# Helical rotation bias: from bias matmuls to a bias operand in the squares and in the normalisation

## The chip, the core and the metric

The kernel runs on one core of a Trainium2 chip. TensorE does matmuls (its results go to PSUM), VectorE and ScalarE do elementwise work on PSUM and SBUF, GpSimd does elementwise work on SBUF alone, and SyncE (SP) starts the DMA transfers. The metric is the device time of the core in microseconds; lower is better. Line numbers (L955) are those of the profiled kernel.

## What is computed

The reference is a stack of two small transformer layers on 1024 tokens of 128 features. The change lies in one of its six blocks, the helical attention of the second layer:

```python
qh = (x @ Wq.T + bq).reshape(b, s, h, hd)          # 16 heads of 8 features; kh the same
q_hel = einsum('bshd,hed->bshe', qh, Whel) + bhel  # 64 helical features a head
n = sqrt(sum(q * q, axis=-1, keepdims=True))       # q_hel taken as 32 pairs; k_hel the same
qn = q / maximum(n, 1e-12)
helical = einsum('bhpsc,bhptc->bhst', scramble(qn), scramble(kn)) / 32
dot = einsum('bshd,bthd->bhst', qh, kh) / sqrt(hd)
attn = softmax(0.5 * dot + 0.5 * helical)
out = einsum('bhst,bthd->bshd', attn, vh) ... @ Wo.T + bo
```

What counts here is `+ bhel` on the rotation's result, the sum of the two squares of a pair, the bound 1e-12 on the norm (1e-24 on its square), and the product with the inverse norm.

## The kernel before

All engines run programs written out by hand; each engine does its instructions in the order of its program, and semaphores join them. No scheduler sets an order. The 1024 tokens are two halves of 512 columns. A bank is one of the eight 128x512 float32 regions of PSUM.

The helical attention runs in eight **turns** `u = 0..7` (`HEL`: half `u // 4`, group of four heads `u % 4`) and two more to drain. In turn u:

- TensorE (the loop under `for u in range(len(HEL) + 2)`): `dots(u, w)` for query and key, then `rotate(u, w, j)` for four **rotations** n = 4u + 2w + j. A rotation fills bank `2 + n % 4` with two halves of 256 columns, c = 0 and 1, the two features of a pair. Each half is one matmul for the bias (L661) and three (`mm3`, L326 to L328) for the product, since each operand is split into a high and a low part for float32 accuracy. Then come the transposes of the softmax weights of turn u-2, the first score product of u-1 (`score`, L683), work for values or projections, the weighing of values for u-2 (L710), and the second score product of u-1. A rotation waits for the bank's last reader (`h_norm`).
- ScalarE: the query's dot bias (L991), the softmax exponential of u-2 (L997), `squares(2u)` and `squares(2u+1)` (L955, a bank each, four in all), `inverse(2u)` (L960 a logarithm, L961 an exponential with scale -0.5: the inverse norm), a copy of turned weights (L1010), `inverse(2u+1)`, and half of the score extraction (L970).
- GpSimd: `add_squares(m)` (L1140), the sum of a pair's squares, once for each of m = 2u and 2u+1; once, in turn 3, the low part of the second half's tokens (`y_rest`, L1096) stands between the two. Before the turns it makes the high and low parts of the weights (L1129, L1132), and ahead of those the memsets for the bias matmuls (L1119 to L1123).
- VectorE: `mask_dot` (L1539, L1540), `softmax_sum` (L1587), `normalise(2u)` (L1564, four STT: scalar-tensor-tensor, which take the smaller of the inverse norm and a bound and multiply by the rotation in PSUM), half of the score extraction (L1549), `normalise(2u+1)`, work for values (L1572) or projections (L1525), `result(u-2)` (L1599), the second extraction, and `softmax_shift(u-1)` (L1580 the maximum, L1582 the subtraction) which releases L997 of the next turn.

The bias comes by DMA as a 34-row tile `hbias` (16 x 128 numbers, each row pair twice) into `wraw` at L294. VectorE splits it into high and low rows (`stage_bias`, L1499 and L1500, in the decoder's first sum), and the bias matmul multiplies those rows, in the zeroed tiles `ph` and `pl`, by rows of ones. The bound of the norm lies in two places: the logarithm's bias `lntiny` (1e-26 after a scale of 2^20) and the minimum with 1e12 in L1564.

## Time and profile before

| | us |
|---|---|
| median of 3 runs (lowest to highest) | 568.51 (567.17 to 570.62) |
| the profiled execution, its own time | 567.71 |
| its span | 565.9 |
| TensorE busy, matmuls | 455.4 (80%) |
| VectorE busy | 421.8 (75%) |
| ScalarE busy | 301.6 (53%) |
| GpSimd busy | 102.3 (18%) |
| helical attention, first rotation to its last result | about 314 to 430 |

The span is what the hardware profiler recorded of one execution; 1.8 us lie around it. Busy time is time in which an engine has an instruction in flight. Instructions of one engine overlap a little: two neighbours' starts may be closer than one's duration, and the start-to-start time is what a row of equal instructions costs each. An entry "xN" in a timeline is N neighbours merged, its time from the first start to the last end. A note in brackets is the idle time ahead of the instruction and the instruction that ended it. "L1564 <- L961" in a list of waits means that the first sat idle for the second.

### The profile page before, as it was taken

What the parts mean: (1) busy time and instruction counts of PE and PEld (TensorE: products, weight loads), DVE (VectorE), ACT (ScalarE), POOL (GpSimd) and SP (SyncE); (2) the same over time, 40 slices, a digit from 0 to 9 for tenths busy, and PEclk for the clock granted to TensorE, in tenths of its full rate; (3) what the DMA queues carried; (4) which work ended last, traced back from release to release, by engine and by line L of the source; (5) the groups of instructions that cost most, each with busy time, mean ns of one, the idle gap of its engine ahead of it and who ended that gap; (6) DMA issues with size and microseconds to landing.
All of it is one profiled execution on the core that took longest, in us unless ns stands there. A gap on an engine that the chain in (4) does not pass through costs nothing.

```text
span 565.9 us, 9003 instructions
## 1 busy us (share of the span) xinstructions
PE 455.4 (80%) x2936; PEld 343.3 (61%) x2953; DVE 421.8 (75%) x1022; ACT 301.6 (53%) x567; POOL 102.3 (18%) x106
## 2 busy tenths in 40 slices
PE   5883327999999999475686979999865579999996
PEld 2442314778778787352344868888754337777774
DVE  3489865777777777668877796778687667888885
ACT  4252134667776675332233567765642227777774
POOL 1000030122211120070000221321100502222220
PEclk9887557999999999757888899999995659999999
DMA  8950001111011100000000000000001110211101
GB/s 311 415 209 0 0 7 50 57 57 56 9 47 56 56 15 2 0 0 2 1 1 2 1 2 2 1 2 2 2 1 38 38 37 1 68 44 37 37 1 37
DMA packets 7566, 24.08 MB, mean 43 GB/s; under 512 B 790, under 2 KB 3014, under 8 KB 7404
## 3 DMA queue, kind: packets, MB, share of 16 engines
q1 hardware_dynamic: 7532, 23.63, 11.5%
q8 instruction: 20, 0.33, 0.2%
q14 instruction: 14, 0.11, 0.1%
HBM read 23.11 MB, written 0.52 MB: 42 GB/s over the span
## 4 chain that ended last, share of the span: by engine, by line
PE 60%; DVE 21%; issue 7%; ACT 6%; DMA 3%; SPq 2%; POOL 1%; DVEq 0%; ACTq 0%; POOLq 0%
PE pair L326 14%; PE pair L327 13%; PE pair L328 13%; DMA arena<-in_zT 3%; PE turn L320 2%; DVE arena L1564 2%; PE pair L683 1%; PE turn L326 1%; DVE work L1382 1%; PE turn L474 1%; PE pair L609 1%; DVE st L1190 1%; ACT YT L807 1%; DVE Y L1213 1%; PE turn L327 1%
## 5 line engine op out<-in xcount | busy, mean ns | idle before, releaser
L326 PE MATMUL pair<-yTh,wh 128*128 128x512 f32 x128 | 61.4, 480 | 4.1 <-issue 3.8
L1047 ACT ACTIVATE work<-pair,vec 128x512 f32<-128x512 f32 x64 | 44.1, 689 | 29.5 <-PE pair L328 24.2
L1671 DVE TENSOR_TENSOR pair<-work,turn 128x512 f32<-128x512 f32 x64 | 44.5, 696 | 17.9 <-ACT work L1047 16.1
L327 PE MATMUL pair<-yTl,wh 128*128 128x512 f32 x128 | 51.9, 405 | 0.0
L328 PE MATMUL pair<-yTh,wl 128*128 128x512 f32 x128 | 51.6, 403 | 0.0
L1419 DVE TENSOR_TENSOR pair<-work,pair 128x512 f32<-128x512 f32 x48 | 33.4, 696 | 23.3 <-PE pair L328 22.0
L1103 POOL TENSOR_TENSOR wl<-wraw,wh 128x512 fp32r<-128x512 f32 x24 | 30.9, 1291 | 97.5 <-ACT wh L878 97.5
L899 ACT ACTIVATE ph<-pair 128x512 fp32r<-128x512 f32 x48 | 28.8, 600 | 27.0 <-DVE pair L1419 27.0
L886 ACT ACTIVATE work<-pair 128x512 f32<-128x512 f32 x64 | 38.3, 598 | 4.5 <-PE pair L328 3.4
L326 PE MATMUL pair<-ph,wh 128*128 128x512 f32 x96 | 38.3, 399 | 0.9 <-DVE pl L1437 0.8
L683 PE MATMUL pair<-arena 64*128 64x128 f32 x512 | 32.9, 278 | 6.3 <-ACT work L970 4.6
L328 PE MATMUL pair<-ph,wl 128*128 128x512 f32 x96 | 37.9, 395 | 0.0
L327 PE MATMUL pair<-pl,wh 128*128 128x512 f32 x96 | 37.8, 393 | 0.0
L1564 DVE SCALAR_TENSOR_TENSOR arena<-work,pair 128x256 f32<-128x256 f32 x64 | 22.6, 416 | 19.1 <-ACT work L961 18.9
L683 PEld LDWEIGHTS pair<-arena 64*128 64x128 f32 x512 | 29.9, 188 | 9.0 <-ACT work L970 6.1
L1140 POOL TENSOR_TENSOR work<-work 128x512 f32<-128x512 f32 x16 | 20.4, 1279 | 76.5 <-ACT work L955 76.5
L320 PE MATMUL turn<-con,Y 128*128 128x128 f32 x56 | 13.0, 379 | 26.1 <-DVE Y L1213 19.6
L1437 DVE TENSOR_TENSOR pl<-pair,ph 128x512 fp32r<-128x512 f32 x48 | 32.8, 684 | 0.1
L807 ACT ACTIVATE YT<-turn 128x512 f32<-128x512 f32 x16 | 9.6, 597 | 43.1 <-PE turn L320 43.1
L1096 POOL TENSOR_TENSOR yTl<-YT,yTh 128x512 fp32r<-128x512 f32 x6 | 7.7, 1278 | 134.9 <-ACT yTh L821 134.9
L326 PEld LDWEIGHTS pair<-yTh,wh 128*128 128x128 f32 x128 | 25.4, 199 | 9.9 <-issue 5.6
L328 PEld LDWEIGHTS pair<-yTh,wl 128*128 128x128 f32 x128 | 24.9, 194 | 6.2
(285 smaller groups left out, 1200.3 us busy)
## 6 DMA issues: line engine op xcount, KB each, us to landing
wraw<-in_w SPq DMA_DIRECT2D x8, 768.0 KB, 4.4
arena<-in_zT SPq DMA_DIRECT2D x8, 514.0 KB, 10.8
arena<-in_z SPq DMA_DIRECT2D x8, 512.0 KB, 11.4
wraw<-in_w SPq DMA_DIRECT2D x8, 512.0 KB, 3.2
mat<-in_mat SPq DMA_DIRECT2D x1, 2312.0 KB, 17.9
row<-in_row SPq DMA_DIRECT2D x1, 576.0 KB, 17.3
X<-in_x SPq DMA_DIRECT2D x1, 512.0 KB, 4.1
out_x<-X SPq DMA_DIRECT2D x2, 256.0 KB, 2.5
```

What stands on the lines that cost most here:

```text
L326: pe.matmul(out, ah, bh, start=start, stop=False)
L327: pe.matmul(out, ah, bl, start=False, stop=False)
L328: return pe.matmul(out, al, bh, start=False, stop=stop)
L683: last = pe.matmul(pair[2][:, j, (2 * i + k) * P:(2 * i + k + 1) * P], a[rows, cols], b[rows, cols], start=n == 0, stop=n == 1, skip_group ...
L886: act.activation(act_out[q % 2], GATE0, ACT.Silu).then_inc(m["act"], 1)
L899: act.activation(ph[q % 2][:, :], UP0[q % 4], ACT.Copy).then_inc(m["hi"], 1)
L1047: act.activation(act_out[q % 2], UP1[q % 4], ACT.Relu, bias=vec[:, bass.ds(at, 1)])\
L1103: pool.tensor_tensor(wl[k][:, cols], wraw[:, cols], wh[k][:, cols].bitcast(F32), ALU.subtract)\
L1419: dve.tensor_tensor(up, act_out[q % 2], up, ALU.mult).then_inc(m["mul"], 1)
L1437: dve.tensor_tensor(pl[q % 2][:, :], UP0[q % 4], ph[q % 2][:, :].bitcast(F32), ALU.subtract)\
L1564: last = dve.scalar_tensor_tensor(out, inv, (QF, 1.0)[m % 2] * 1e12, src, ALU.min, ALU.mult)
L1671: dve.tensor_tensor(UP1[q % 4], act_out[q % 2], bank[h], ALU.mult).then_inc(m["mul"], 1)
```

## The change

The bias no longer passes through TensorE. A new tile `bhel` (128 x 16) holds it as columns, one for each rotation half. Two DMA loads of 4-byte pieces fill it at the start, on SP's queue between the parameters and the first expert weights. ScalarE squares each half of a bank by itself, with `bhel`'s column as the activation's bias; VectorE's STT adds the same column to the rotation and multiplies by the inverse norm. The bound of the norm is a maximum with 1e-24 on GpSimd behind each sum of squares, with a semaphore `h_sum2` between the two. The bias matmuls, their staging on VectorE, their memsets on GpSimd, `lntiny` and the old load are gone.

```diff
+            for r, c, n in ((0, 0, W0C // P), (32, W0C // P, NH - W0C // P)):
+                sp.dma_start(bhel[:, c:c + n], d["hbias"][r, 0:n * P].rearrange("(k p) -> p k", p=P),
+                             allow_slow_non_contiguous=True).then_inc(bias_loaded, 16)
...
-                    sp.dma_start(wraw[0:34, :], d["hbias"]).then_inc(bias_loaded, 16)
...
                 for c in range(2):
-                    bias, one = hel_bias(2 * pr + c)
                     o = bank[2 + n % 4][:, c * 256:(c + 1) * 256]
-                    pe.matmul(o, bias, one, start=True, stop=False)
                     last = mm3(o, whel(wh, 2 * pr + c), whel(wl, 2 * pr + c), qe_h(h, w)[:, cols], qe_l(h, w)[:, cols],
-                               False, True)
+                               True, True)
...
                     act.wait_ge(h_hel, n + 1)
-                    act.activation(sq(m)[:, j * HN:(j + 1) * HN], bank[2 + n % 4], ACT.Square).then_inc(h_sq, 1)
+                    for c in range(2):
+                        at = j * HN + c * 256
+                        last = act.activation(sq(m)[:, at:at + 256], bank[2 + n % 4][:, c * 256:(c + 1) * 256],
+                                              ACT.Square, bias=hel_bias(n, c))
+                    last.then_inc(h_sq, 1)
...
-                step(act.activation(n2(m), n2(m), ACT.Ln, scale=float(2 ** 20), bias=lntiny[:, :]))
+                step(act.activation(n2(m), n2(m), ACT.Ln, scale=float(2 ** 20)))
...
-            for b in bias_at:
-                pool.memset(b[:, :].bitcast(F32), 0.0)
-            pool.memset(ones[:, :].bitcast(F32), 0.0).then_inc(pool_step, 1)
-            pool.wait_ge(pool_step, 2)
-            for r in (0, 32):
-                pool.memset(ones[r:r + 2, 8 * r:8 * r + 256].bitcast(F32), 1.0).then_inc(bias_zero, 1)
...
                 pool.tensor_tensor(n2(m).rearrange("p (j m) -> p j m", j=2), s4[:, :, 0], s4[:, :, 1], ALU.add)\
-                    .then_inc(h_n2, 1)
+                    .then_inc(h_sum2, 1)
+                pool.wait_ge(h_sum2, m + 1)
+                pool.tensor_scalar(n2(m), n2(m), 1e-24, None, ALU.max).then_inc(h_n2, 1)
...
-            def stage_bias():
-                dve.wait_ge(bias_loaded, 16)
-                dve.wait_ge(bias_zero, 2)
-                for c, b in enumerate(bias_at):
-                    raw = wraw[0:34, c * HN:(c + 1) * HN]
-                    step(dve.tensor_copy(b[0:34, :], raw))
-                    last = dve.scalar_tensor_tensor(b[0:34, :], b[0:34, :].bitcast(F32), ccol("biaslo")[0:34, :], raw,
-                                                    ALU.mult, ALU.add)
-                last.then_inc(h_bias, 1)
...
-                        last = dve.scalar_tensor_tensor(out, inv, (QF, 1.0)[m % 2] * 1e12, src, ALU.min, ALU.mult)
+                        last = dve.scalar_tensor_tensor(out, src, hel_bias(n, c), inv, ALU.add, ALU.mult)
```

ScalarE and VectorE wait for the two loads once, ahead of the turns. What stands on ScalarE in turn 3, from the softmax exponential to the second inverse step, before:

```order
L997 ACTIVATE work<-work 128x512 [waits h_sub]
L955 ACTIVATE work<-pair 128x512 [waits h_hel,h_n2]
L955 ACTIVATE work<-pair 128x512 [waits h_hel]
L955 ACTIVATE work<-pair 128x512 [waits h_hel,h_n2]
L955 ACTIVATE work<-pair 128x512 [waits h_hel]
L960 ACTIVATE work<-work,lntiny 128x512 [waits h_n2]
L961 ACTIVATE work<-work,cq 128x512 [waits act_step]
```

and now, in the same turn:

```order
L999 ACTIVATE work<-work 128x512 [waits h_sub]
L954 ACTIVATE work<-pair,bhel 128x256 [waits h_hel,h_n2]
L954 ACTIVATE work<-pair,bhel 128x256
L954 ACTIVATE work<-pair,bhel 128x256 [waits h_hel]
L954 ACTIVATE work<-pair,bhel 128x256
L954 ACTIVATE work<-pair,bhel 128x256 [waits h_hel,h_n2]
L954 ACTIVATE work<-pair,bhel 128x256
L954 ACTIVATE work<-pair,bhel 128x256 [waits h_hel]
L954 ACTIVATE work<-pair,bhel 128x256
L961 ACTIVATE work<-work 128x512 [waits h_n2]
L962 ACTIVATE work<-work,cq 128x512 [waits act_step]
```

Four squares have become eight, and the logarithm has lost its bias operand. On GpSimd, from the first sum to the end of the sums, before:

```order
L1140 TENSOR_TENSOR work<-work 128x512 [waits h_sq] x2
L1140 TENSOR_TENSOR work<-work 128x512 [waits h_norm,h_sq] x5
L1096 TENSOR_TENSOR yTl<-YT,yTh 128x512 [waits y_hi]
L1140 TENSOR_TENSOR work<-work 128x512 [waits h_norm,h_sq] x9
L1096 TENSOR_TENSOR yTl<-YT,yTh 128x512 [waits y_hi] x2
```

and now, around turn 3:

```order
L1134 TENSOR_TENSOR work<-work 128x512 [waits h_norm,h_sq]
L1137 TENSOR_SCALAR work<-work 128x512 [waits h_sum2]
L1097 TENSOR_TENSOR yTl<-YT,yTh 128x512 [waits y_hi]
L1134 TENSOR_TENSOR work<-work 128x512 [waits h_norm,h_sq]
L1137 TENSOR_SCALAR work<-work 128x512 [waits h_sum2]
```

Each sum has a maximum behind it, and every later instruction of GpSimd stands behind both.

## Rows read from the trace of the kernel before

**Rows 1.** Windows: us, then busy us (instructions) of PE, PEld, DVE, ACT, POOL; PEclk.

```profile
367.00:380.00 13.00, 12.46 (x179) 11.22 (x177) 10.69 (x30) 8.14 (x15) 2.37 (x3) 1.00 0.01 3
...
407.00:420.00 13.00, 10.34 (x137) 9.30 (x137) 8.59 (x22) 7.82 (x15) 2.56 (x2) 1.00 0.01 1
```

**Rows 2.** Waits, 310 to 430 us: total us, times, longest.

```profile
DVE arena L1564 <- ACT work L961: 18.9, 9, 3.8
```

**Rows 3.** Timeline of VectorE, turn 4: start, us, instruction [idle before].

```profile
363.77 0.69 DVE L1582 TENSOR_TENSOR work<-work,hstat 128x512 f32<-128x512 f32 x1
...
369.04 1.42 DVE L1564 SCALAR_TENSOR_TENSOR arena<-work,pair 128x256 f32<-128x256 f32 x4 [2.14 <-ACT work L961]
370.37 0.84 DVE L1549 COPY work<-pair 32x256 f32<-32x256 f32 x2
371.24 1.42 DVE L1564 SCALAR_TENSOR_TENSOR arena<-work,pair 128x256 f32<-128x256 f32 x4
...
374.16 1.17 DVE L1599 TENSOR_TENSOR Y<-turn,hstat 32x128 f32<-32x128 f32 x4
...
376.96 0.69 DVE L1582 TENSOR_TENSOR work<-work,hstat 128x512 f32<-128x512 f32 x1
```

**Rows 4.** Timeline of ScalarE, turn 4.

```profile
364.49 0.63 ACT L997 ACTIVATE work<-work 128x512 f32<-128x512 f32 x1 [1.50 <-DVE work L1582]
365.03 1.73 ACT L955 ACTIVATE work<-pair 128x512 f32<-128x512 f32 x3
367.05 0.60 ACT L955 ACTIVATE work<-pair 128x512 f32<-128x512 f32 x1 [0.29 <-PE pair L328]
367.54 0.71 ACT L960 ACTIVATE work<-work,lntiny 128x512 f32<-128x512 f32 x1
368.29 0.72 ACT L961 ACTIVATE work<-work,cq 128x512 f32<-128x512 f32 x1
```

**Rows 5.** Timeline of GpSimd, turns 3 and 4.

```profile
354.46 1.29 POOL L1096 TENSOR_TENSOR yTl<-YT,yTh 128x512 fp32r<-128x512 f32 x1
...
366.18 1.28 POOL L1140 TENSOR_TENSOR work<-work 128x512 f32<-128x512 f32 x1 [9.20 <-ACT work L955]
367.72 1.27 POOL L1140 TENSOR_TENSOR work<-work 128x512 f32<-128x512 f32 x1 [0.26 <-ACT work L955]
```

**Rows 6.** Timeline of TensorE, the last rotation of turn 4.

```profile
366.37 0.29 PE L661 MATMUL pair<-pl,ph 128*128 128x256 f32 x1
366.49 0.28 PE L326 MATMUL pair<-arena_r,wh 128*128 128x256 f32 x1
```

**Rows 7.** Timeline of ScalarE, turn 2: an activation of 128x256 with a bias column.

```profile
346.34 0.84 ACT L977 ACTIVATE arena_r<-turn,vec 128x256 fp32r<-128x256 f32 x2
```

**Rows 8.** Timeline of VectorE, turn 2: an STT with a column, from PSUM.

```profile
347.21 0.88 DVE L1525 SCALAR_TENSOR_TENSOR arena_r<-turn,vec,arena_r 128x256 fp32r<-128x256 f32 x2 [0.41 <-ACT arena_r L977]
```

**Rows 9.** Groups of GpSimd by line and form: busy us, mean ns, idle us before.

```profile
L1158 POOL CAST wh<-wraw 128x512 fp32r<-128x512 f32 x16 | 9.4, 616 | 69.2 <-PE pair L328 65.6 <-DMA wraw<-in_w 3.6
```

**Rows 10.** Timeline of ScalarE, turn 6.

```profile
392.74 2.04 ACT L955 ACTIVATE work<-pair 128x512 f32<-128x512 f32 x4
395.19 0.72 ACT L960 ACTIVATE work<-work,lntiny 128x512 f32<-128x512 f32 x1 [0.41 <-POOL work L1140]
```

**Rows 11.** Timeline of ScalarE and VectorE, turn 7.

```profile
408.25 0.60 ACT L955 ACTIVATE work<-pair 128x512 f32<-128x512 f32 x1 [0.29 <-PE pair L328]
...
410.24 1.42 DVE L1564 SCALAR_TENSOR_TENSOR arena<-work,pair 128x256 f32<-128x256 f32 x4 [3.25 <-ACT work L961]
```

**Rows 12.** Timeline of VectorE, turn 0.

```profile
321.28 2.91 DVE L1564 SCALAR_TENSOR_TENSOR arena<-work,pair 128x256 f32<-128x256 f32 x8 [2.55 <-ACT work L961]
```

**Rows 13.** Timeline of ScalarE, decoder's second half.

```profile
296.02 0.28 ACT L814 ACTIVATE ry<-mv,eps 128x4 f32<-128x4 f32 x1
```

**Rows 14.** The line L878: duration min/median/max in ns, first and last start.

```profile
L878 ACT ACTIVATE wh<-wraw x24: 612/624/634, 79.0 to 203.3; 128x512 fp32r<-128x512 f32 x24
```

**Rows 15.** The page, part 2: DMA busy in tenths, 40 slices.

```profile
DMA  8950001111011100000000000000001110211101
```

More of the change, by code:

```diff
@@ L101, in build @@
         omt, tdn, step_bias = sb("omt", [P, 3]), sb("tdn", [P, 1]), sb("step_bias", [P, 2])
-        hstat, lntiny = sb("hstat", [P, 48]), sb("lntiny", [P, 1])
+        hstat, bhel = sb("hstat", [P, 48]), sb("bhel", [P, NH])
         eps = sb("eps", [P, 1])
@@ L194, in build, with hel_bias @@
         vb = lambda t: vb_at[t]
-        bias_at, ones = [ph[0], ph[1], pl[0]], pl[1]
-        def hel_bias(k):
-            r, c = (0, k) if k < 12 else (32, k - 12)
-            return blk(bias_at[c // 4], c % 4), ones[:, 8 * r:8 * r + 256]
+        def hel_bias(n, c):
+            pr = 2 * HEL[n // 4][1] + n % 2
+            return bhel[:, 2 * pr + c:2 * pr + c + 1]
         def own_banks(rows):
@@ L237, in build @@
         f_h, f_relu, f_out, f_sum = (sem("f_" + n) for n in ("h", "relu", "out", "sum"))
-        h_w, bias_loaded, h_bias, bias_zero = sem("h_w"), sem("bias_loaded"), sem("h_bias"), sem("bias_zero")
-        h_e, h_eh, h_ec, h_hel, h_sq, h_n2, h_inv, h_norm, h_d, h_dq, h_dk, h_v, h_vb = (
-            sem("h_" + n) for n in ("e", "eh", "ec", "hel", "sq", "n2", "inv", "norm", "d", "dq", "dk", "v", "vb"))
+        h_w, bias_loaded = sem("h_w"), sem("bias_loaded")
+        h_e, h_eh, h_ec, h_hel, h_sq, h_sum2, h_n2, h_inv, h_norm, h_d, h_dq, h_dk, h_v, h_vb = (
+            sem("h_" + n) for n in ("e", "eh", "ec", "hel", "sq", "sum2", "n2", "inv", "norm", "d", "dq", "dk", "v", "vb"))
         h_s, h_sxa, h_sxd, h_sub, h_exp, h_sum, h_et, h_ets, h_pv, h_o, h_out, h_x = (
@@ L740, in _ @@
             pe.wait_ge(h_w, 1)
-            pe.wait_ge(h_bias, 1)
             for u in range(len(HEL) + 2):
@@ L981, in _ @@
             copy_turned(yt(0))
+            act.wait_ge(bias_loaded, 32)
             for w in range(2):
@@ L1074, in _ @@
             pool.memset(cq[:, :], LN2 * 10 + math.log(QF))
-            pool.memset(lntiny[:, :], 1e-26)
             pool.memset(eps[:, :], EPS).then_inc(eps_ready, 1)
@@ L1117, in _ @@
             pool.wait_ge(tok_ready, 8)
-            for b in bias_at:
-                pool.memset(b[:, :].bitcast(F32), 0.0)
-            pool.memset(ones[:, :].bitcast(F32), 0.0).then_inc(pool_step, 1)
-            pool.wait_ge(pool_step, 2)
-            for r in (0, 32):
-                pool.memset(ones[r:r + 2, 8 * r:8 * r + 256].bitcast(F32), 1.0).then_inc(bias_zero, 1)
-            pool.wait_ge(bias_zero, 2)
             parts = [(wh[0][:, :], wl[0][:, :], mcol("Whel", 0, W0C)),
@@ L1129, in _ @@
                 pool.tensor_copy(hi, w).then_inc(pool_step, 1)
-            pool.wait_ge(pool_step, 6)
+            pool.wait_ge(pool_step, 5)
             for hi, lo, w in parts:
@@ L1508, in decoder_sum @@
                 step(dve.tensor_tensor(v, v, along("b2"), ALU.add))
-                if h == 0:
-                    stage_bias()
                 dve.wait_ge(f_out, h + 1)
@@ L1610, in add_out @@
                 dve.tensor_tensor(half(X, h), bank[1], half(X, h), ALU.add).then_inc(h_x, 1)
-            dve.wait_ge(h_bias, 1)
+            dve.wait_ge(bias_loaded, 32)
             for u in range(len(HEL) + 2):
```

## Prediction

> **What bounds the kernel now.** I read the page's 40 slices first, to find the stage that the change touches. The helical attention runs from about 310 to 430 us of the 565.9 us span; everything else in the diff is a load at the start, a little work of GpSimd and VectorE in the stages before. The stage is eight turns u = 0..7 (two halves of the tokens times four groups of heads), and from turn 3 on a turn takes about 13.1 us. The busy time by stretch [rows 1] says TensorE: 12.46 of 13.00 us busy in turn 4, at full clock. By that alone, taking matmuls away looks like a gain. But a busy TensorE can be one that is paced by others, so I then read who waits, and VectorE waits 18.9 us in nine waits for one thing, ScalarE's second step of the inverse norm (L961) [rows 2]. So I walked one turn on each engine.
>
> On VectorE [rows 3] the turn closes into a loop. The softmax shift L1582 ends at 364.46 (363.77 plus 0.69). Normalising of the next unit, L1564, starts at 369.04, after 2.1 us of idle time; between them lie only 2.5 us of other work. Then come four STT (1.33 to the next start), two copies (0.87), four STT (1.33), the value blocks, the result (L1599), two copies, the maximum and the shift again, which ends at 377.65: 13.19 later, with nothing idle from 369.04 on. What fills the 4.58 us from shift to normalising is ScalarE [rows 4]: exponential L997 at 364.49, squares L955 from 365.03, the fourth square at 367.05, logarithm L960 at 367.54, exponential L961 at 368.29 to 369.01. Two paths end at that logarithm together. One is TensorE's: the fourth square waited 0.29 for the last rotation. The other is GpSimd's: the sum of the first two squares ran from 366.18 to 367.46 [rows 5], 0.08 before the logarithm. In turn 6 ScalarE's squares run without a wait and the logarithm waits 0.41 for GpSimd [rows 10]. So there are three ties: TensorE, ScalarE's queue and GpSimd each set the turn to within 0.3 us.
>
> **TensorE: 64 bias matmuls go.** Starts of neighbours are 0.12 apart (366.37, 366.49) [rows 6], so a turn loses 8 x 0.12 = 0.95 us of TensorE, 7.6 us in all. Only the fourth square waits for that, and it is 0.3 us before the next bound. I take nothing for it in turns 3 to 6, where the path below gets longer than TensorE's.
>
> **ScalarE: each square becomes two halves with a bias operand.** The nearest row has exactly this shape, PSUM to SBUF, 128x256, bias from a column: two of L977 take 0.84 with 0.47 for one [rows 7], so start to start is 0.37. GpSimd needs the first four halves: 3 x 0.37 + 0.47 = 1.58 us from the first start. Before, two whole squares took about 1.08 (2.04 for four less two further steps of 0.48 [rows 10]). That is **+0.50** ahead of GpSimd. All eight take 3.06 against 2.04, or 2.6 with the wait for TensorE. Bounds: a half costs no less than half a whole square's 0.56 (then +0.05 in place of 0.50) and no more than 0.47 with no overlap (+0.8).
> The Trainium skill ("ScalarE: Activation LUTs", What ACT_TABLE_LOAD costs) states that a [128,1] pointer operand adds about 93 ns to an activation, with a fixed part besides the time per element and 93 ns of overlap back to back; by it a half would be about 0.49 with 0.40 start to start, an estimate, and this term +0.6. The trace's 0.47 and 0.37 nearly agree, and the sum goes by the trace.
> The logarithm loses its bias operand. Same size without one is L997's 0.63, against L960's 0.71 [rows 4]: **-0.08** on the path.
>
> **GpSimd: a maximum behind each sum.** The trace has no such operation. One input, one output, 128x512 is the cast L1158 at 0.61; two inputs is the sum itself, 1.28 [rows 5, 9]. I take 0.61, since the maximum against a constant has one input like the cast, and 0.08 for the wait on the engine's own semaphore: **+0.69**. Upper end 1.28 + 0.08. Nothing excludes a little less than the cast, but the same tile must be read and written, so I keep it as the lower end.
> The Trainium skill ("GPSIMD Engine Reference", 4.1 Engine selection) says that elementwise work such as a maximum belongs on VectorE, since two-input operations are some two times slower on GpSimd, while one-input ones run roughly at line rate. Here the rows show 1.28 against VectorE's 0.69 for two inputs, as it says, and 0.61 for one. Taken as one-input the sum keeps 0.69; taken as two-input it would be 1.36.
> Queued behind the maximum is the next sum. Sum, maximum, sum, maximum end 2.22 + 2 x (1.26 + 0.69) = 6.1 after the shift; logarithm 2 and exponential 2 then end at 7.6. VectorE wants that at 5.66 + 1.60 + 0.87 = 8.1. So the second inverse stays hidden, except in turn 3, where the remainder of y (L1096, 1.24 [rows 5]) stands between the two sums: there it comes at 8.9 and VectorE waits 0.8. Before, that turn lost about 0.5 at the same place, so +0.3.
>
> **VectorE: normalising takes a bias column.** L1564 runs at 0.335 start to start (1.42 for four with 0.42 for one) [rows 3]. L1525 is an STT of 128x256 with source PSUM, a column and an SBUF tensor, the new form: 0.88 for two with 0.48 for one [rows 8], so 0.40. Eight per turn, all on the loop: 8 x 0.065 = **+0.52**. Lower end 0; upper 0.6.
>
> **The sum for a turn.** In turns 4, 5 and 6: 0.50 + 0.69 - 0.08 + 0.52 = 1.6 us each, 4.9 in all. Check that nothing gained on TensorE comes off: its last rotation now ends 0.95 earlier relative to VectorE's result, and ScalarE's last half runs from about 3.2 after the shift, when TensorE has long delivered, so TensorE now idles. Turn 3: 1.6 + 0.3 = 1.9. The first turns have no softmax ahead of the squares, and the squares waited for TensorE each time, so TensorE's gain pays for ScalarE's halves there. What is left in turn 0 is the second inverse: VectorE's eight STT ran in one piece, 2.91 from 321.28 [rows 12]; now, by the prices above, the first sum starts near 317.8, the second maximum ends near 321.8, the inverse at 323.2, and the last STT ends 0.8 later. Turn 1 hides more, turn 2 adds 0.2 (its last square is late by 0.75 on ScalarE behind the copy of turned tokens, of which most is carried over): 1.0 together. Turn 7 was TensorE's: the fourth square at 408.25 waited for it, normalising began at 410.24 [rows 11]. With 0.95 less there, ScalarE's halves end at 408.3, GpSimd's maximum at 408.8, so the start stays, but eight slower STT remain: +0.5. Sum: 1.0 + 1.9 + 4.9 + 0.5 = **+8.3 us**.
>
> **Elsewhere: nothing.** VectorE loses six staging instructions in the decoder's first sum, but what follows waits for ScalarE's L814, which at 296.02 starts with no idle time behind a relu [rows 13]: it can't come sooner because its input does. At most 0.1. GpSimd loses six memsets ahead of the weights' high and low parts, long before the turns. Two loads of 4-byte pieces, 2048 of them, now stand on SP's queue ahead of the first expert weights; the queue delivers in order of issue, so the inputs ahead of them are safe. The DMA engines fall idle in the fourth slice, from about 42 us [rows 15], and ScalarE first reads those weights at 79.0 [rows 14]. That cover is 37 us; without it each piece would count.
>
> **Rivals.**
> (a) TensorE was the bound after all: it is 96% busy [rows 1] and sets the fourth square. Then each turn gets 0.95 shorter and the kernel takes 568.5 - 7.6 = 561 us. Against it: in turn 6 nothing waited for it and the turn was no shorter. It needs the halves, the maximum and the STT all hidden. 6%.
> (b) The small prices are at their lower ends: STT no dearer (-3.2 over all turns) and halves at 0.28 (-2.1). Then +3, 571.5; with some gain from TensorE in turns 1 and 7 about 570. 13%.
> (c) The maximum costs what a sum costs: +0.67 on the first inverse in turns 4 to 6, double in turn 3 and in the first turns where both inverses count, some 5.5 us in all: 582. It decides from 0.9 us up, when the second inverse comes later than 8.1. 12%.
> (d) TensorE, idle some 3 us more per turn, is granted the lower clock in a turn or two. Its 11.5 us of work per turn would take nearly twice as long, about 6 us more per turn: 589. Against it: in turn 7 it was busy 10.34 of 13 us and kept 1.00 [rows 1], the share I expect now. 4%.
> (e) The forecast, +5 to +11: 65%.
>
> **How the numbers follow.** The profiled execution took 567.71; plus 8.3 is 576.0. The median of the runs was 568.51, 0.8 above, so 576.8 by it; I give 576.5. Range: low end case (b) at 570.5, high end case (c) with halves at 0.47, 583; that leaves out (a), (d) and part of (b). About 0.5% (2.8 us) is what a measurement of this kernel tells from no change: faster 0.07, same 0.11 (most of b), slower 0.82.
>
> **What would show it.** After the change: VectorE's wait for ScalarE's second inverse step grows from 2.1 to some 3.2 us a turn in turns 3 to 6, and ScalarE's logarithm waits for GpSimd in them; TensorE's busy time in a turn falls under 11.7 of about 14.7; the maximum reads 0.6; the STT 0.48; a half square 0.47; the squares no longer wait for TensorE. I am wrong if the turn stays at 13.1, or if the maximum reads over 0.9.

## The result and the profile after

The changed kernel takes **593.9 us** (median of 4 runs, 592.61 to 595.56) against 567.84 us for the kernel before (566.51 to 570.62) measured beside it: a ratio of 1.0454 [1.04, 1.0507]. It is slower, as forecast, but by three times as much: 26.1 us in place of 8, and the time lies above the top of the range. The profiled execution took 592.61 us, its span is 590.8.

First the page. Busy time and instructions by engine, then the chain of work that ended last:

```profile
PE 460.2 (78%) x2889; PEld 344.8 (58%) x2889; DVE 423.5 (72%) x1016; ACT 307.1 (52%) x599; POOL 123.0 (21%) x115
...
PE 55%; DVE 21%; POOL 8%; ACT 8%; issue 4%; DMA 3%; SPq 1%; DVEq 0%; ACTq 0%; POOLq 0%
PE pair L326 12%; PE pair L328 12%; PE pair L327 12%; POOL work L1137 4%; POOL work L1134 3%; DMA arena<-in_zT 3%; PE pair L681 2%; ACT work L954 2%; PE turn L320 2%; PE turn L474 1%; DVE st L1186 1%; PE pair L609 1%; PE turn L326 1%; DVE work L1378 1%; PE pair L339 1%
```

GpSimd is busy for 21% of the span and still has 8% of the chain; the new maximum, L1137, is its largest part with 4% of the span. Which stage that is, the waits of the turns (314 to 450 us) tell; columns as in [rows 2]:

```profile
DVE arena L1548 <- ACT work L962: 33.4, 16, 4.3
ACT work L961 <- POOL work L1137: 20.9, 16, 2.2
```

VectorE's wait for the inverse norm has grown from 18.9 us in nine waits [rows 2] to 33.4 in sixteen: now it waits for both inverses of every turn, where the second one used to be hidden. ScalarE's logarithm waits for the maximum all sixteen times. The lines of the new instructions; durations min/median/max in ns, then first and last start:

```profile
L1137 POOL TENSOR_SCALAR work<-work x16: 1483/1484/1489, 323.3 to 433.1; 128x512 f32<-128x512 f32 x16
L1134 POOL TENSOR_TENSOR work<-work x16: 1262/1269/1290, 322.0 to 431.7; 128x512 f32<-128x512 f32 x16
L954 ACT ACTIVATE work<-pair,bhel x64: 456/482/522, 320.3 to 429.8; 128x256 f32<-128x256 f32 x64
L1548 DVE SCALAR_TENSOR_TENSOR arena<-pair,bhel,work x64: 473/476/484, 326.3 to 437.2; 128x256 f32<-128x256 f32 x64
```

Halves (0.48) and STT (0.476) came as [rows 7] and [rows 8] had them. The maximum takes **1.48 us**, where I took 0.61 and had 1.28 as the upper end.

The same turn as in [rows 3] to [rows 5], now between the shift that ends at 377.23 and the next, 15.95 later. ScalarE:

```profile
377.26 0.63 ACT L999 ACTIVATE work<-work 128x512 f32<-128x512 f32 x1 [1.49 <-DVE work L1566]
377.80 3.01 ACT L954 ACTIVATE work<-pair,bhel 128x256 f32<-128x256 f32 x8
382.30 0.63 ACT L961 ACTIVATE work<-work 128x512 f32<-128x512 f32 x1 [1.50 <-POOL work L1137]
382.96 0.72 ACT L962 ACTIVATE work<-work,cq 128x512 f32<-128x512 f32 x1
383.59 0.58 ACT L1012 ACTIVATE work<-turn 128x512 f32<-128x512 f32 x1
385.11 0.63 ACT L961 ACTIVATE work<-work 128x512 f32<-128x512 f32 x1 [0.94 <-POOL work L1137]
385.77 0.72 ACT L962 ACTIVATE work<-work,ck 128x512 f32<-128x512 f32 x1
```

GpSimd:

```profile
379.43 1.27 POOL L1134 TENSOR_TENSOR work<-work 128x512 f32<-128x512 f32 x1 [9.59 <-ACT work L954]
380.79 1.48 POOL L1137 TENSOR_SCALAR work<-work 128x512 f32<-128x512 f32 x1
382.24 1.27 POOL L1134 TENSOR_TENSOR work<-work 128x512 f32<-128x512 f32 x1
383.59 1.48 POOL L1137 TENSOR_SCALAR work<-work 128x512 f32<-128x512 f32 x1
```

VectorE:

```profile
376.54 0.69 DVE L1566 TENSOR_TENSOR work<-work,hstat 128x512 f32<-128x512 f32 x1
...
383.72 1.66 DVE L1548 SCALAR_TENSOR_TENSOR arena<-pair,bhel,work 128x256 f32<-128x256 f32 x4 [4.05 <-ACT work L962]
385.30 0.83 DVE L1533 COPY work<-pair 32x256 f32<-32x256 f32 x2
386.52 1.66 DVE L1548 SCALAR_TENSOR_TENSOR arena<-pair,bhel,work 128x256 f32<-128x256 f32 x4 [0.40 <-ACT work L962]
...
392.49 0.69 DVE L1566 TENSOR_TENSOR work<-work,hstat 128x512 f32<-128x512 f32 x1
```

Read as one path, against the turn before: shift to first sum 1.72 before, 2.20 now (+0.48, the halves); sum to logarithm 1.36, now 2.87 (+1.51, the maximum); logarithm to the start of normalising 1.50, now 1.42 (-0.08). Then, on VectorE, the first four STT to the second four 2.20, now 2.80 (+0.60: 0.24 for four slower STT and a new wait of 0.40, since the second inverse ends at 386.49, less a little), and from there to the end of the shift 6.41, now 6.66 (+0.25, STT again). The sum is +2.76, where I had 1.6.

The whole stage, from the remainder of y on GpSimd to the end of the last shift, took 112.7 us before (310.80 to 423.53) and takes 133.7 (315.08 to 448.81): **+21.0**. The other 3.9 of the 24.9 us between the two spans lie ahead of the turns (+4.3) and behind them (-0.4). The lengths below run from the end of one shift to the next in the timelines of VectorE; "stage" is as just said. Turns 0 and 1 (up to the first shift's end) and the drain behind turn 7 are in the stage and have no column.

| kernel | turn 2 | 3 | 4 | 5 | 6 | 7 | stage |
|---|---|---|---|---|---|---|---|
| before | 14.52 | 12.96 | 13.19 | 14.51 | 12.50 | 12.62 | 112.7 |
| after | 16.18 | 16.47 | 15.95 | 17.28 | 16.27 | 15.86 | 133.7 |
| before + maximum (e2) | 16.07 | 16.13 | 15.34 | 16.68 | 14.92 | 15.29 | 132.4 |
| after, copy for maximum (e6) | 14.58 | 14.65 | 14.68 | 16.02 | 14.03 | 13.13 | 119.7 |
| after, times one (e13) | 15.81 | 16.48 | 15.97 | 17.31 | 17.59 | 16.26 | 135.6 |
| before + halves (e3) | 14.75 | 13.43 | 13.63 | 14.96 | 12.99 | 12.87 | 115.3 |
| before + column STT (e4) | 14.51 | 12.95 | 13.68 | 15.01 | 12.98 | 13.09 | 115.0 |
| before - matmuls (e9) | 14.02 | 12.96 | 13.15 | 14.46 | 12.49 | 11.75 | 109.6 |
| after - maximum (e1) | 14.25 | 13.32 | 14.02 | 15.35 | 13.62 | 12.45 | 114.7 |
| after, maximum on VectorE (e12) | 14.66 | 16.47 | 14.53 | 15.85 | 13.88 | 12.96 | 122.8 |
| after, bias in the parameter tile (e5) | 16.00 | 16.48 | 15.95 | 17.29 | 15.31 | 16.14 | 133.1 |

The granted clock of TensorE, 1.00 for 2.4 GHz and 0.50 for 1.2, in the same stretches, is used further down (the labels are those of the experiments below):

| kernel | turns 0 and 1 | 2 | 3 | 4 | 5 | 6 | 7 |
|---|---|---|---|---|---|---|---|
| before | 0.93 | 1.00 | 1.00 | 1.00 | 1.00 | 1.00 | 1.00 |
| after | 0.83 | 1.00 | 0.90 | 0.89 | 1.00 | 0.79 | 0.89 |
| e5 | 0.83 | 1.00 | 0.90 | 0.89 | 1.00 | 1.00 | 0.89 |
| e13 | 0.89 | 1.00 | 0.90 | 0.89 | 0.90 | 0.81 | 0.79 |
| e10 (zeros multiplied) | 0.89 | 1.00 | 1.00 | 0.89 | 0.90 | 0.80 | 0.90 |
| e6 | 0.94 | 1.00 | 1.00 | 1.00 | 0.89 | 1.00 | 1.00 |

### The profile page after: what moved, and what is told of

It is laid out like the page before. It is cut to its first block, busy times and chain, and to the rows that moved or that the text cites. A ratio compares the mean times of both kernels' runs of the same rounds, so it can differ in the third digit from the quotient of the medians.

```text
span 590.8 us, 8931 instructions
## 1 busy us (share of the span) xinstructions
PE 460.2 (78%) x2889; PEld 344.8 (58%) x2889; DVE 423.5 (72%) x1016; ACT 307.1 (52%) x599; POOL 123.0 (21%) x115
## 2 busy tenths in 40 slices
DMA packets 9610, 23.87 MB, mean 40 GB/s; under 512 B 2868, under 2 KB 5092, under 8 KB 9448
## 4 chain that ended last, share of the span: by engine, by line
PE 55%; DVE 21%; POOL 8%; ACT 8%; issue 4%; DMA 3%; SPq 1%; DVEq 0%; ACTq 0%; POOLq 0%
PE pair L326 12%; PE pair L328 12%; PE pair L327 12%; POOL work L1137 4%; POOL work L1134 3%; DMA arena<-in_zT 3%; PE pair L681 2%; ACT work L954 2%; PE turn L320 2%; PE turn L474 1%; DVE st L1186 1%; PE pair L609 1%; PE turn L326 1%; DVE work L1378 1%; PE pair L339 1%
## 5 line engine op out<-in xcount | busy, mean ns | idle before, releaser
L1415 DVE TENSOR_TENSOR pair<-work,pair 128x512 f32<-128x512 f32 x48 | 33.4, 696 | 24.4 <-PE pair L328 23.7
L1548 DVE SCALAR_TENSOR_TENSOR arena<-pair,bhel,work 128x256 f32<-128x256 f32 x64 | 26.5, 477 | 33.4 <-ACT work L962 33.4
L681 PE MATMUL pair<-arena 64*128 64x128 f32 x512 | 37.6, 303 | 10.2 <-ACT work L971 6.3
L681 PEld LDWEIGHTS pair<-arena 64*128 64x128 f32 x512 | 34.5, 212 | 13.2 <-ACT work L971 8.3
L328 PEld LDWEIGHTS pair<-yTh,wl 128*128 128x128 f32 x128 | 24.9, 194 | 6.2
## 6 DMA issues: line engine op xcount, KB each, us to landing
mat<-in_mat SPq DMA_DIRECT2D x1, 2312.0 KB, 17.8
row<-in_row SPq DMA_DIRECT2D x1, 576.0 KB, 17.4
```

Source lines behind the costliest of these rows:

```text
L328: return pe.matmul(out, al, bh, start=False, stop=stop)
L681: last = pe.matmul(pair[2][:, j, (2 * i + k) * P:(2 * i + k + 1) * P], a[rows, cols], b[rows, cols], start=n == 0, stop=n == 1, skip_group ...
L1415: dve.tensor_tensor(up, act_out[q % 2], up, ALU.mult).then_inc(m["mul"], 1)
```

## The experiments

Each is named by its label; ratios are against the kernel before, in runs beside it, with a 95% interval.

**The maximum alone, added to the kernel before.** Is it the maximum, or the parts together?

```diff
-                    .then_inc(h_n2, 1)
+                    .then_inc(h_sum2, 1)
+                pool.wait_ge(h_sum2, m + 1)
+                pool.tensor_scalar(n2(m), n2(m), 1e-24, None, ALU.max).then_inc(h_n2, 1)
```

> The kernel before with only the maximum and its wait added behind each sum on GpSimd (bias matmuls, whole squares and the old STT stay). Theory M: first inverse 1.5 later; sum, maximum, sum, maximum end 7.35 after the softmax shift, so the second inverse is 0.5 late too: 2.0 a turn in about seven turns, 582. Rival S: under 575.

Measured: 589.99 us, 1.0357 [1.0325, 1.0389]; the stage +19.6. GpSimd and VectorE of this kernel in turn 4:

```profile
379.89 1.27 POOL L1140 TENSOR_TENSOR work<-work 128x512 f32<-128x512 f32 x1
381.24 1.49 POOL L1143 TENSOR_SCALAR work<-work 128x512 f32<-128x512 f32 x1
...
384.27 1.42 DVE L1566 SCALAR_TENSOR_TENSOR arena<-work,pair 128x256 f32<-128x256 f32 x4 [0.64 <-ACT work L961]
```

One more instruction on GpSimd for each sum brings nearly four fifths of the loss in time and 19.6 of the 21.0 us of the stage, with the same 1.49 and a late second inverse too (0.64). It is more than the 582 expected: turns 0 and 1 lost 3.8, turn 3 lost 3.2 and the drain behind turn 7 lost 1.7, where 2.0 in some seven turns had been counted. In that drain, where the granted clock was 0.79, VectorE waited 2.55 for 32 score matmuls that took 3.79 us; at 1.00 they take 2.06.

**The changed kernel without the maximum**, with the bound of the norm left out.

```diff
-                    .then_inc(h_sum2, 1)
-                pool.wait_ge(h_sum2, m + 1)
-                pool.tensor_scalar(n2(m), n2(m), 1e-24, None, ALU.max).then_inc(h_n2, 1)
+                    .then_inc(h_n2, 1)
```

> The changed kernel without GpSimd's maximum (the bound on the norm is left out of the computation; the sum of squares releases ScalarE directly). Theory M: the maximum, 1.48 us and a wait of 0.08 in series on the inverse norm, twice a turn, is most of the loss: each turn from 3 to 6 gets 1.5 (first inverse) + 0.4 (second inverse no longer late) = 1.9 shorter, the first turns and turn 7 some 2 each, 14 to 16 us in all, so 578 to 580. Rival S: the loss comes from the start (the loads of 4-byte pieces) and from TensorE's clock: then 588 or more stays.

Measured: 572.52 us over 10 runs, 1.0027 [0.9998, 1.0056]; the stage +1.9. All the rest of the change together is a tie or a very small loss: turn 4 loses 0.83 and turn 7 gains 0.17. The expectation of 578 to 580 was too high, since 19.1 us of the stage came back and not 14 to 16: 4.0 in turns 0 and 1, 3.2 in turn 3 and 3.4 in turn 7, against 1.9 in turns 2, 4 and 5.

**A copy in the maximum's place.** Same tile, same place, same wait, but a form that costs what I had taken. The bound is left out here too.

```diff
-                pool.tensor_scalar(n2(m), n2(m), 1e-24, None, ALU.max).then_inc(h_n2, 1)
+                pool.tensor_copy(n2(m), n2(m)).then_inc(h_n2, 1)
```

> The changed kernel with a plain copy in place on GpSimd where the maximum stands (the bound is left out of the computation). If one input and one output set the price, as the prediction held, the copy too costs 1.48 and the time stays at 594. If the price belongs to the form of a tensor-scalar operation, the copy costs about 0.61 as the cast does and each turn gets 0.87 shorter on the first inverse plus 0.4 on the second: 580 to 584.

Measured: 578.71 us, 1.016 [1.0112, 1.0207]; the stage +7.0. The copy's group on GpSimd, 310 to 460 us: busy us, mean ns, idle us before.

```profile
L1137 POOL COPY work<-work 128x512 f32<-128x512 f32 x16 | 9.8, 610 | 1.0
```

So the forecast's sum holds for the price that it was made with, and so does its sign on VectorE: the wait for the first inverse in turn 4 is 3.15 here, where I had 3.2. The time is a little under the 580 to 584 that I expected of this run. Stretch by stretch: turns 0 to 2 +0.3 (forecast 1.0), turn 3 +1.7 (1.9), turns 4 to 6 +4.5 (4.9), turn 7 +0.5 (0.5): +7.0 against 8.3. The changed kernel's stage is 14.0 longer than this one's, and sixteen times the difference of price, 0.87, is 13.9. That the two agree so closely is chance, since by turns it is not so even: turn 0 +1.9, turn 2 +1.6 and turn 3 +1.8, about 0.87 for each maximum in them; turn 1 +1.2, where VectorE's work for values hides a part; turns 4 and 5 +1.3 each, 0.87 for the first and the wait of 0.40 for the second; turns 6 and 7 +2.2 and +2.7, more than both maxima (why, below).

**Times one in the maximum's place.** Is 1.48 the price of a maximum, or of the form? The bound is left out.

```diff
-                pool.tensor_scalar(n2(m), n2(m), 1e-24, None, ALU.max).then_inc(h_n2, 1)
+                pool.tensor_scalar(n2(m), n2(m), 1.0, None, ALU.mult).then_inc(h_n2, 1)
```

> The changed kernel with a multiplication by 1.0 in place of the maximum with 1e-24 (the bound is left out of the computation). If 1.48 us is the price of GpSimd's tensor-scalar form, it stays and the time is that of the changed kernel, 592 to 595. If it is the price of a maximum, it falls towards the copy's 0.61 and the time to 578 to 582.

Measured: 591.86 us, 1.0373 [1.0329, 1.0418]. The group:

```profile
L1137 POOL TENSOR_SCALAR work<-work 128x512 f32<-128x512 f32 x16 | 23.8, 1490 | 1.4
```

1.49 for a multiplication. It is the form, a tile with an immediate scalar on GpSimd, and not the operation.

**The halves alone**, in the kernel before, with a column of zeros as bias.

```diff
-                    act.activation(sq(m)[:, j * HN:(j + 1) * HN], bank[2 + n % 4], ACT.Square).then_inc(h_sq, 1)
+                    for c in range(2):
+                        at = j * HN + c * 256
+                        last = act.activation(sq(m)[:, at:at + 256], bank[2 + n % 4][:, c * 256:(c + 1) * 256],
+                                              ACT.Square, bias=zcol[:, :])
+                    last.then_inc(h_sq, 1)
```

> The kernel before with each square as two halves of 128x256 with a bias column of zeros (the matmuls still add the bias). Term of the prediction: +0.5 a turn where GpSimd's sum sets the logarithm, less where TensorE did: 570 to 571.5. If each half costs its full 0.48, 573.

Measured: 576.65 us, 1.0117 [1.0087, 1.0148]. ScalarE in turn 4:

```profile
371.20 3.01 ACT L957 ACTIVATE work<-pair,zcol 128x256 f32<-128x256 f32 x8
```

Turn 4 grows by 0.44, the stage by 2.6, near 0.50 a turn. The ratio says more, 5 to 8 us, and the time is above the 570 to 571.5 expected. The rest lies ahead of the turns, which begin at 315.94 in this execution, though all code before them but one memset is the same: between 60 and 100 us the granted clock was 0.51 here and 0.61 in the kernel before. That is taken up under "what stays open".

**The new form of the STT alone**, with a column of zeros, in the kernel before; the minimum with 1e12 and the factor 2^-10 are left out.

```diff
-                        last = dve.scalar_tensor_tensor(out, inv, (QF, 1.0)[m % 2] * 1e12, src, ALU.min, ALU.mult)
+                        last = dve.scalar_tensor_tensor(out, src, zcol[:, :], inv, ALU.add, ALU.mult)
```

> The kernel before with VectorE's normalising in the new form: source plus a column (of zeros) times the inverse norm; the minimum with the bound is left out. Term of the prediction: 0.065 x 8 = 0.5 a turn on VectorE's loop: 571 to 572. If it is hidden: 568.

Measured: 572.89 us over 10 runs, 1.0059 [1.0032, 1.0087]. In turn 4 VectorE shows

```profile
370.82 1.66 DVE L1565 SCALAR_TENSOR_TENSOR arena<-pair,zcol,work 128x256 f32<-128x256 f32 x4 [2.14 <-ACT work L961]
```

and the turn is 0.49 longer, for eight STT 0.06 dearer; the wait ahead is the 2.14 of [rows 3], unchanged. The stage +2.3.

**The bias matmuls gone alone**, from the kernel before; the bias is left out of the result.

```diff
-                    pe.matmul(o, bias, one, start=True, stop=False)
                     last = mm3(o, whel(wh, 2 * pr + c), whel(wl, 2 * pr + c), qe_h(h, w)[:, cols], qe_l(h, w)[:, cols],
-                               False, True)
+                               True, True)
```

> The kernel before with the 64 bias matmuls taken out and all else kept (the rotation's bias is left out of the computation). The prediction took nothing for them in turns 3 to 6 and about 1 us each in turns 0, 1 and 7: 566 to 568. If TensorE was the bound of each turn (rival a): 0.95 a turn, 561 to 562.

Measured: 566.81 us over 10 runs, 0.9951 [0.9918, 0.9983]; the stage -3.1 of the 7.6 us of matmuls. ScalarE in turn 4, then VectorE:

```profile
366.73 2.04 ACT L954 ACTIVATE work<-pair 128x512 f32<-128x512 f32 x4
369.18 0.72 ACT L959 ACTIVATE work<-work,lntiny 128x512 f32<-128x512 f32 x1 [0.41 <-POOL work L1139]
...
370.69 1.42 DVE L1563 SCALAR_TENSOR_TENSOR arena<-work,pair 128x256 f32<-128x256 f32 x4 [2.09 <-ACT work L960]
```

The squares now run through without the 0.29 of [rows 4], and the logarithm waits 0.41 for GpSimd instead: the tie of three, seen from the other side. Turns 3 to 6 keep their length to 0.05; turn 2 (-0.50), turn 7 (-0.87) and the first two (-1.6) gain. The four parts alone make 19.6 + 2.6 + 2.3 - 3.1 = 21.4; together they were measured at 21.0. They add up to within 1 us only: 1.7 of the 19.6 is e2's drain, which the changed kernel doesn't lose, and without the drains the parts make 20.0.

**Bias columns in the parameter tile**, so that the two loads of 4-byte pieces go; all else as in the changed kernel.

```diff
-            for r, c, n in ((0, 0, W0C // P), (32, W0C // P, NH - W0C // P)):
-                sp.dma_start(bhel[:, c:c + n], d["hbias"][r, 0:n * P].rearrange("(k p) -> p k", p=P),
-                             allow_slow_non_contiguous=True).then_inc(bias_loaded, 16)
...
-            return bhel[:, 2 * pr + c:2 * pr + c + 1]
+            return vcol("bhel", 2 * pr + c)
```

> The changed kernel with the bias columns laid into the parameter tile vec that is loaded anyway, in place of the two loads of 4-byte pieces. Theory M (the loads are hidden, the turns carry the loss): within 2 us of the changed kernel, 592 to 595. Rival S (the 4 us by which the turns began later in the changed kernel's profile come from the loads): 589 to 590, with the turns' start back near 311 us.

Measured: 590.38 us, 1.0394 [1.0344, 1.0443], against 1.0454 [1.04, 1.0507] with the loads. In the changed kernel SP's queue shows what they are:

```profile
18.99 14.36 SPq L289 DMA_DIRECT2D bhel<-in_hbias  x2
33.40 2.78 SPq L296 DMA_DIRECT2D wraw<-in_w  x1
```

The issue of the two took 14.36 us, and the first expert weights, issued at 18.78 in the kernel with bias columns in the parameter tile, now go out at 33.40. The cover of 37 us that I had read held, less a part: ScalarE first reads those weights at 80.5 in the changed kernel, with no idle time ahead of it, and in the executions without the loads at 78.1 to 82.3. The stage of e5 is 133.1, and its turns begin at 314.1 where the rival wanted 311. By the times of the runs up to some 3 us of loss is neither shown nor excluded, since the intervals overlap, but no trace shows a wait for it. The inputs ahead of the loads were safe: the large piece of the matrices landed 17.8 us after its issue (17.9 before), the row tile after 17.4 (17.3).

**Zeros multiplied where the bias matmuls were**, to keep TensorE as busy as before. Rival (d) said that the clock would fall because TensorE has less to do.

```diff
+                    pe.matmul(o, blk(ph[0], 0), pl[1][:, 0:256], start=True, stop=False)
                     last = mm3(o, whel(wh, 2 * pr + c), whel(wl, 2 * pr + c), qe_h(h, w)[:, cols], qe_l(h, w)[:, cols],
-                               True, True)
+                               False, True)
```

> The changed kernel with 64 matmuls of zeros put where the bias matmuls stood (they add nothing to the result). TensorE has idle time in each turn, so by theory M their 0.12 us each is hidden and only the granted clock can answer: if the lower clock that the changed kernel shows in some turns costs time there, keeping TensorE busier gives back 2 to 5 us, 588 to 591, with PEclk 1.00 in all turns; if the clock is harmless, 594 to 596.

Measured: 593.33 us, 1.0415 [1.0374, 1.0456], the stage 136.3; no gain that can be told. The same window, first of the changed kernel, then of this one; columns as in [rows 1]:

```profile
390.00:405.00 15.00, 11.47 (x176) 10.44 (x174) 10.34 (x26) 8.92 (x19) 5.46 (x4) 1.00 0.01 2
```

```profile
390.00:405.00 15.00, 12.87 (x176) 12.04 (x175) 10.37 (x28) 7.90 (x18) 5.47 (x4) 0.89 0.01 3
```

TensorE is busier by an eighth, and its clock is not higher (0.89 for 1.00). One window is not enough, since the clock of a turn differs between executions: by the table of the clock above, e10 is higher than the changed kernel in turns 0, 1 and 3, lower in turn 5 and the same elsewhere, and e13, which has no such matmuls, differs from the changed kernel as much. Eight matmuls more in a turn do not hold it up at 1.00.

**Both maxima on VectorE**, ahead of the first normalising of the turn, with the bias columns in the parameter tile. If the form is dear on GpSimd only, most comes back.

```diff
-                pool.wait_ge(h_sum2, m + 1)
-                pool.tensor_scalar(n2(m), n2(m), 1e-24, None, ALU.max).then_inc(h_n2, 1)
...
+                    bound(2 * u)
+                    bound(2 * u + 1)
                     normalise(2 * u)
```

> The changed kernel (bias columns in vec) with both maxima of a turn on VectorE, in the 4 us in which it waits for the inverse norm. A maximum there should take 0.3 to 0.7; the first inverse then comes 0.9 later than in the kernel before, not 1.9, and the second is never late: turn of 14.5 to 14.8, 576 to 580. Rival: a hand-over from GpSimd to VectorE to ScalarE and a VectorE in order eat the gain, 585 or more.

Measured: 579.55 us, 1.0166 [1.0127, 1.0205]. VectorE, then GpSimd, in turn 4:

```profile
377.68 0.43 DVE L1547 TENSOR_SCALAR work<-work 128x512 f32<-128x512 f32 x1 [1.06 <-POOL work L1130]
379.27 0.43 DVE L1547 TENSOR_SCALAR work<-work 128x512 f32<-128x512 f32 x1 [1.16 <-POOL work L1130]
```

```profile
376.38 1.27 POOL L1130 TENSOR_TENSOR work<-work 128x512 f32<-128x512 f32 x1 [12.57 <-ACT work L951]
377.84 1.40 POOL L1130 TENSOR_TENSOR work<-work 128x512 f32<-128x512 f32 x1 [0.20 <-ACT work L951]
```

0.43 in place of 1.48, and 11.0 of the 21.0 us of the stage come back. VectorE stands still for 1.16 between the two, since its queue is in order and the second sum ends only at 379.24. Turn 3 stays at 16.47, 3.2 longer than without a maximum (e1), and the first two turns are 2.8 longer than there: 6 of the 8.1 us by which the two stages differ. GpSimd, then VectorE, in turn 3:

```profile
361.14 1.26 POOL L1093 TENSOR_TENSOR yTl<-YT,yTh 128x512 fp32r<-128x512 f32 x1
```

```profile
361.21 1.48 DVE L1547 TENSOR_SCALAR work<-work 128x512 f32<-128x512 f32 x1 [1.06 <-POOL work L1130]
```

Here the same maximum took 1.48 on VectorE too: it started 0.07 behind the remainder of y on GpSimd and ended 0.29 after it. Normalising begins 1.55 later in that turn than in e1. The other 1.6 is TensorE's: its second scores took 3.19 us, at a granted clock of 0.50 from 366 to 369.5 us and 0.74 to 372.5, and VectorE waited 1.73 for them. In the first two turns 2.2 of the 2.8 us fall in turn 1, where both maxima stood in VectorE's queue behind its work for values; the first began at 332.75, though its sum had ended at 330.32. For that turn the place that I chose is a poor one; another was not tried.

**Squares ahead of the softmax exponential.** The changed kernel without GpSimd's maximum (the bound back in the logarithm's bias, bias columns in the parameter tile), with the first two squares on ScalarE before L997's exponential; and the same order in the kernel before, as its control.

```diff
+                if u < len(HEL):
+                    squares(2 * u)
                 if u >= 2:
                     act.wait_ge(h_sub, u - 1)
...
-                    squares(2 * u)
```

> A candidate: the changed kernel with the bound back in the logarithm's bias (no maximum on GpSimd), the bias columns in vec, and ScalarE's first pair of squares ahead of the softmax exponential, where ScalarE idled 1.5 us a turn. The first sum can start about 1 us sooner after the shift; the logarithm then waits for ScalarE's second pair: level with the kernel before at best, 566 to 572. If the order makes no difference: 572 to 575 as without the maximum.

> The kernel before with only the order on ScalarE changed: the first pair of squares ahead of the softmax exponential. The fourth square still waits for TensorE's last rotation in most turns, so the logarithm starts no sooner: 568 to 570. If ScalarE's queue set the turn and not TensorE: 564 to 566.

Measured: 569.89 us over 10 runs, 1.0033 [1.0004, 1.0062]; the control 567.65, 0.9982 [0.9951, 1.0012]. ScalarE of the first of the two ahead of turn 5 shows where the gain ends:

```profile
378.58 1.57 ACT L951 ACTIVATE work<-pair,vec 128x256 f32<-128x256 f32 x4 [1.17 <-PE pair L325]
380.02 0.64 ACT L997 ACTIVATE work<-work 128x512 f32<-128x512 f32 x1
```

The squares waited 1.17 for the rotation, so here the order only exchanges one wait for another. It does better where the turn waited for GpSimd and not for TensorE: turn 6 of the control takes 11.22 in place of 12.50, and its stage 111.1 in place of 112.7, less than its times can tell. The kernel before was beaten beyond the interval only by e9, which leaves the bias out.

## Why the prediction was wrong

The direction and the stage were right, and so was the path that a maximum lengthens. Its price was not, and with it went the point and the range: 576.5 (570.5 to 583) against 593.9. By its steps:

- **What bounds the kernel: right.** A 96% busy TensorE [rows 1] was not what the turn hangs on. Taking its matmuls away left turns 3 to 6 alone (e9), as "I take nothing for it in turns 3 to 6" had it. Rival (a), 561, is out. In turns 0 to 2 and 7 it gives 2.9 us, which I had set against the halves there; with the copy (e6) those turns come to +0.8 where I had 1.5.
- **ScalarE's halves +0.50: right.** Turn 4 gives 0.48 in the changed kernel and 0.44 alone (e3). First sum 2.20 after the shift, forecast 2.22. The Trainium skill's 93 ns for a pointer operand ("ScalarE: Activation LUTs", What ACT_TABLE_LOAD costs) agrees with the logarithm, 0.63 without and 0.71 with [rows 4].
- **Logarithm -0.08: right.**
- **VectorE's STT +0.52: right in size** (eight x 0.06 = 0.49, e4).
- **GpSimd's maximum +0.69: the step that failed.** I reasoned "the maximum against a constant has one input like the cast", and took the cast's 0.61 [rows 9]. It measured 1.48, and 1.57 with the wait ahead of it, so my own sign of being wrong, a maximum over 0.9, came true. I should have seen that neither row was of its form: a cast and a sum of two tiles bound it only if the engine's time goes by the number of inputs. It doesn't: 0.61 for a copy with one input (e6), 1.49 for one input and a constant (e13), 1.27 for two inputs. My upper end, 1.28, was the price of another form again and no bound. The Trainium skill ("GPSIMD Engine Reference", 4.1 Engine selection) puts a maximum on VectorE and calls one-input work on GpSimd roughly line rate; the trace agrees with the copy and with the advice, and not with line rate for this form, where 1.48 against VectorE's 0.43 decides.
- **"The second inverse stays hidden": fell with it.** Rival (c) names the condition, a price over 0.9, when the second inverse comes later than VectorE wants it. It came 9.26 after the shift where 8.1 was forecast as the limit and VectorE in fact wanted it at 8.9. So GpSimd stands in the path twice a turn. The 0.9 itself was too low, for it kept 8.1 fixed although a dearer maximum delays VectorE as well; by the same sum the second inverse comes out of hiding at 1.1 (7.6 + 2 x 0.5 = 8.1 + 0.5). For turn 3 I had said that it lost about 0.5 there before; the trace has a wait of 0.29. (c) had the mechanism, but at its price it gave 582; at the real one the stage is 14.0 us above e6's.
- **Turns 0 to 2: +1.0 forecast, +5.0 measured.** Turns 0 and 1, from 310.80 to the first shift's end at 336.98 before, took 26.18; now, 315.08 to 344.58, 29.50. With a copy (e6) they take 26.46. In turn 0 VectorE has no other work between the two groups of STT that would hide a second inverse, and waited 1.16 for it: both maxima lie on the path (+1.9 against e6). In turns 1 and 2 it waited 0.18 and 0.41 for it; I had worked out turn 0 alone.
- **Rival (d), the clock: it fell, for a small part of the loss.** The clock was under 1.00 in most turns of the changed kernel, and cost time only where VectorE waited for TensorE: turn 3 took 16.47 at 0.90, and in e10 16.47 at 1.00. Rows of the changed kernel in turns 6 and 7: TensorE's scores, the windows around them, and VectorE's extractions behind them.

```profile
420.56 3.04 PE L681 MATMUL pair<-arena 64*128 64x128 f32 x32 [0.28 <-ACT work L971]
...
436.84 3.41 PE L681 MATMUL pair<-arena 64*128 64x128 f32 x32 [1.95 <-ACT work L971]
```

```profile
417.00:424.00 7.00, 6.26 (x48) 5.84 (x49) 5.42 (x15) 3.46 (x7) 1.31 (x1) 0.60 0.00 0
434.00:441.00 7.00, 4.30 (x40) 3.92 (x39) 5.03 (x15) 2.79 (x6) 0.58 (x1) 0.76 0.00 0
```

```profile
423.65 0.84 DVE L1533 COPY work<-pair 32x256 f32<-32x256 f32 x2 [1.14 <-PE pair L681]
...
440.30 0.84 DVE L1533 COPY work<-pair 32x256 f32<-32x256 f32 x2 [1.51 <-PE pair L681]
```

At 2.4 GHz these 32 matmuls take 2.06 us (turn 4, at 379.16). With part of the window at the lower level they took 3.04 and 3.41, and in both turns they began behind ScalarE's L971, which stands behind the late second exponential. VectorE waited 1.14 and 1.51 for them. About that much these turns lost beyond what turn 4 did, each against e6: 2.24 - 1.27 = 0.97 and 2.73 - 1.27 = 1.46. Ahead of the first TensorE had idled 3.63 us for ScalarE's L1012, up to 417.46, and ahead of the second 2.01, up to 433.74; L1012 is the copy of turned weights that now stands behind the late first inverse. The idle time alone does not decide it. Turn 6 of e5, which has the same instructions, idled as long and kept 1.00:

```profile
416.54 0.66 PE L317 MATMUL turn<-con,Y 128*128 128x128 f32 x4 [3.64 <-ACT work L1008]
...
419.65 2.06 PE L678 MATMUL pair<-arena 64*128 64x128 f32 x32 [1.56 <-ACT work L968]
```

That turn took 15.31 against 16.27, so the lower clock cost 0.96 in turn 6. In turn 7 it cost at most 1.35, which is 3.41 less 2.06. So (d)'s mechanism was there and cost some 2 us, not the 12 of (d); in e6 the clock was 0.89 in turn 5 and that turn lost no more than its neighbours. Since e10's extra matmuls did not hold the clock up, what would is not shown.
- **"Elsewhere: nothing": not shown wrong.** In the stage are 21.0 of the 26.1 us. The times of e5 leave room for up to some 3 us for the loads, and no trace shows them.

**What stays open.** The rest is where the turns begin. Over the executions with the two loads (the changed kernel, e1, e6, e10, e13) they begin at 312.7 to 316.9 us, mean 314.8; over the nine without them at 310.8 to 315.9, mean 313.4. The kernel before had the earliest of all, and its code up to there is that of e2, e3, e4, e9 and e8b, 312.1 to 315.9. Executions of the same code differ by some 4 us ahead of the turns; in the window from 60 to 100 us the granted clock differs with them. So 1.5 us lie between the two means, which the scatter does not let me tell from nothing, and the 4 us by which e3's ratio goes beyond its turns are of the same kind. The scatter is there early: in e3 ScalarE reads the first expert weights at 82.3, in the kernel before at 79.0. In the six executions of the same code the order by that clock (0.61, 0.60, 0.56, 0.55, 0.53, 0.51) is the order by which the turns begin (310.80 to 315.94). That doesn't say which is the cause, since later work would also lower the mean of a fixed window, and in the executions of the changed code the order does not hold. It is seen, with no cause found.

## What to carry to other kernels

A price for a new operation is to be taken from a row of the same form on the same engine, and where there is none, the nearest rows are no bounds: a form of its own can lie outside both, here at 1.48 us above 0.61 and 1.27. Where the forecast names the price from which a hidden path comes out of hiding, and no row holds that price down, the range must reach to the far side of it. And work moved off an engine that is merely paced, 7.6 us of matmuls here for 3.1 us of time, should not be paid for with new steps on the path that paces it.

## What the runs showed of the hardware

- A tile with an immediate scalar on GpSimd, 128x512, fp32 in SBUF: 1.48 us for a maximum (e2, after), 1.49 for a multiplication (e13). A copy of the same tile there: 0.61 (e6); the sum of two: 1.27. The same maximum on VectorE: about 0.43 in fifteen of sixteen cases and 1.48 in one (e12).
- GpSimd's sum took 1.40 instead of 1.27 when VectorE's maximum ran beside it (e12). The Trainium skill ("GPSIMD Engine Reference", section 1) says that the SBUF interfaces of the two engines are shared; the row agrees in its sign. In turn 3 it went the other way round: VectorE's maximum started 0.07 behind an instruction of GpSimd that took 1.26, and itself took 1.48. Where the two overlapped, the one that started second was the longer one: GpSimd's second sum took 1.39 to 1.42 in turns 0 and 4 to 7, where VectorE's maximum was ahead, and 1.27 in turns 1 and 2, where none ran beside it.
- An instruction of GpSimd that waits for the engine's own semaphore starts 0.06 (the copy of e6) to 0.09 us (the maximum of the changed kernel) after the end of the one ahead.
- Two loads of 2,048 pieces of 4 bytes together held SP's issue for 14.36 us (13.06 to 13.38 in the four other executions that have them); the load of expert weights behind them took 2.78, and 1.08 without them (e5). Packets under 512 B went from 790 to 2868 on the two pages, 2,078 more.
